# The edge masks of a graph kernel are loaded in five parts, each with its own semaphore

## The chip, the cores and the metric

One core of one Trainium2 chip runs the whole program. The metric is device microseconds (us) of one execution; lower is better. The kernel before took 2149.53 us (median of 3 runs, 2148.34 to 2161.56).

The core has five engines with an instruction queue each: TensorE (PE; its weight loads are shown as PEld), VectorE (DVE), ScalarE (ACT), GpSimd (POOL) and SyncE (SP). An engine runs its own instructions in order and waits for the others on semaphores. SP here does nothing but issue transfers (DMAs) between the device memory and the on-chip memory; sixteen DMA engines carry them out.

## The reference: what is computed

50,000 nodes with 128 features each, 12,500 edges sorted by their destination. A first graph convolution, then four layers of graph attention; each of the five adds something to a node from its few incoming edges, and most nodes have none. Cut to what matters:

```python
def _L0_gnn_ref(...):
    msg = node[edge_src] * edge_weight[:, None]
    N_h = segment_sum(msg, edge_dst, num_segments=N_NODES) * in_sqrt_degree
    out = (entity_embed + N_h) @ W_weight.T + W_bias
    return where(out >= 0, out, NEG_SLOPE * out)

def _gat_layer(x, src, dst, ea, W, We, a_s, a_d, a_e, b, g, beta):
    h = x @ W
    alpha = leaky_relu((h @ a_s)[src] + (h @ a_d)[dst] + (ea @ We) @ a_e, 0.2)
    alpha = _segment_softmax(alpha, dst, N)
    out = segment_sum(h[src] * alpha[:, None], dst, num_segments=N) + b
    return layernorm(out) * g + beta

x = x + _L0_gnn_ref(relu(layernorm(x)), ...)
h = relu(layernorm(x))
x = x + (four times _gat_layer, starting from h)
```

The sums over edges of one destination (`segment_sum`) are what the edge masks are for.

## The kernel before, in words

**Edges.** The edges are cut into 100 tiles (`C`) of 125 edges (`P`), and the tiles are worked on two at a time: 50 pairs (`NU`). `S` holds the rows of the source nodes of all edges, `T` those of the destination nodes. In each tile a mask of 125 x 125 says which edges have the same destination; `M` holds the 100 masks in bf16, 12,500 values (25,000 bytes) on each of 125 partitions. For a pair, `mask(n)` multiplies two masks by the weights of their edges into one of four slots (`MA`, `NS` = 4), and TensorE multiplies the rows in `S` by them, which sums edges of one destination.

**Nodes.** The dense part works on all nodes in 100 groups of 500, read from the input into a ring of 12 buffers (`X`, `XS` = 12) and written to the output from there. It is cut into five shares of 36, 16, 16, 16 and 16 groups.

**Stages.** The program is: setup; masks made and stored to memory (`m_t`); `dense` with 36 groups; `conv_layer` over the 50 pairs; and then four times `dense` with 16 groups and `attention(l)`. `attention(l)` has two blocks: first a softmax over all edges, a chain of small operations that goes back and forth between VectorE, TensorE and ScalarE; then a loop over the 50 pairs like that of `conv_layer`. All five engines meet at a barrier at the end of each block.

**Why the masks come back.** The ring `X` and the masks `M` lie on the same bytes (both begin at the start of `R`). So each `dense` overwrites the masks, and they are read back from `m_t` behind it: once at the start of the block of `conv_layer` (line 1266), and once in the softmax block of each `attention(l)` (line 1650), where SP also waits for them to land before it goes to the barrier. In `conv_layer` it is `mask(0)` on VectorE that waits for them (line 1461).

**Transfers.** `dma2` (lines 171 to 173) issues each transfer as two: partitions 0 to 111, and 112 to 124. The two add 16 each to one semaphore, so that 32 says that both have landed.

**Order on the engines.** The loops over pairs are software pipelines: in step `t` each engine does operation `op` for pair `t - lag`, in the order in which `run_slot` is given them. On VectorE in `conv_layer`, in step 2, `mask(0)` stands behind the first steps' statistics, and everything later on VectorE stands behind it. SP issues in `conv_layer` first the masks, and then for each pair a store of its rows once they are ready.

Of the kernel before, what the change touches and what calls it, by code (L numbers as in the profile page):

```python
# [6 lines left out]
BF16 = mybir.dt.bfloat16  # L7
# [8 lines left out]
P = 125  # L16
C = E // P
# [7 lines left out]
XS = 12  # L25
# [8 lines left out]
def gnn_kernel(nc, x, src, dst, ea, ew, w0, b0, wg, we, att_s, att_d, att_e, bg, gamma, beta, out):  # L34
    ctx = ExitStack()
    with ctx:
# [5 lines left out]
        def sem(name):  # L42
            return ctx.enter_context(nc.semaphore(name))
# [12 lines left out]
        def signal(*names):  # L56
            for n in names:
                if n not in signals:
                    signals[n] = Signal(n)
            got = [signals[n] for n in names]  # L60
            return got if len(got) > 1 else got[0]
# [11 lines left out]
        R = RB[0:P]  # L73
# [6 lines left out]
        M = R[:, 0:P * C // 2].bitcast(BF16).rearrange("p (c e) -> p c e", c=C)  # L80
# [82 lines left out]
        row_t = nc.dram_tensor("row_t", [P * TC, RW], F32, kind="Internal").ap()  # L163
        x1_t = nc.dram_tensor("x1_t", [P * TC, D], F32, kind="Internal").ap()
        m_t = nc.dram_tensor("m_t", [P, C * P], BF16, kind="Internal").ap()
        row_v = row_t.rearrange("(p c) f -> p c f", p=P)
        x1_v = x1_t.rearrange("(p c) f -> p c f", p=P)
        x_v = x.rearrange("(i p r) f -> i p r f", p=P, r=Q)
# [2 lines left out]
        def dma2(eng, dst_ap, src_ap, s):  # L171
            eng.dma_start(dst_ap[0:CORE], src_ap[0:CORE]).then_inc(s, 16)
            eng.dma_start(dst_ap[CORE:P], src_ap[CORE:P]).then_inc(s, 16)
# [665 lines left out]
        def dense(first_group, groups, moves, move, arrive):  # L839


            loaded = [signal(f"x_loaded_{s}") for s in range(XS)]
            stored = [signal(f"out_stored_{s}") for s in range(XS)]
            (counted1, var1, rooted1, inverted1, scaled1, y1_vector, y1_scalar, turned1, copied1, conv_done, sloped,
             leaked, joined, counted2, var2, rooted2, inverted2, scaled2, y2_vector, y2_scalar, turned2, copied2,
             beta_added) = signal(
# [390 lines left out]
        def first_moves(pool, a, b):  # L1237
            gather_x(pool, T, dstI, a, b, s_xdst)

        dense(0, SHARES[0], TC, first_moves, [(s_xsrc, 16 * C), (s_xdst, 16 * TC)])  # L1240

        s_ml = sem("masks_loaded")
        s_x1 = sem("x1_stored")
        s_rows = sem("rows_stored")
        STORE = 5
# [2 lines left out]
        def conv_layer():  # L1248
# [14 lines left out]
            with nc.Block() as block:  # L1263
                @block.sync
                def _(sp):
                    dma2(sp, R[:, 0:P * C // 2].bitcast(BF16), m_t, s_ml)
                    for n in range(NU):
                        sp.wait_ge(*beta_added.at(n + 1))
                        dma2(sp, x1_v[:, 2 * n:2 * n + 2, :], XB[:, n % NS, :, :], x1_kept[n % NS].s)
                        if n % STORE == STORE - 1:  # L1270
                            sp.wait_ge(*score_kept.at(n + 1))
                            dma2(sp, row_v[:, 2 * (n + 1 - STORE):2 * n + 2, :], T[:, 2 * (n + 1 - STORE):2 * n + 2, :], s_rows)
                    sp.wait_ge(*x_stage.at(10))
                    sp.dma_start(x1_v[0:C, C, :], END[:, :]).then_inc(s_x1, 16)
                    sp.wait_ge(*x_stage.at(12))
                    sp.dma_start(row_v[:, C, :], T[:, C, :]).then_inc(s_x1, 16)
                    sp.wait_ge(s_x1, 32)
                    for k in range(NS):
                        sp.wait_ge(*x1_kept[k].at(32 * ((NU - k + NS - 1) // NS)))
                    sp.wait_ge(s_rows, 32 * STORES)  # L1280
# [142 lines left out]
                def _(dve):  # L1423
# [33 lines left out]
                        return op  # L1457

                    def mask(n):
                        if n == 0:  # L1460
                            dve.wait_ge(s_ml, 32)
                        if n >= NS:
                            dve.wait_ge(*gathered.at(n - NS + 1))
                        nc.vector.tensor_tensor(MA[:, n % NS, :, :], M[:, 2 * n:2 * n + 2, :],
                                                alphaS[:, 2 * n:2 * n + 2].unsqueeze(2).broadcast_to([P, 2, P]),
                                                ALU.mult).then_inc(masked.s, 1)
# [26 lines left out]
                    for t in slots:  # L1493
                        run_slot(t, NU, [(0, statistics1), (8, keep_scores), (6, scale2), (7, copy2), (5, statistics2), (0, aggregate1), (6, edge), (5, aggregate2), (1, invert1), (2, mask), (4, leak), (1, scale1), (5, invert2)])
# [37 lines left out]
            x_stage.base += 12  # L1532
            x_act.base += 5
            x_pe.base += 5

        conv_layer()

        s_refresh = sem("s_refreshed")
# [9 lines left out]
        def attention(l):  # L1548
# [7 lines left out]
            with nc.Block() as block:  # L1556
# [90 lines left out]

                @block.sync
                def _(sp):
                    dma2(sp, R[:, 0:P * C // 2].bitcast(BF16), m_t, s_ml)  # L1650
                    sp.wait_ge(s_ml, 32 * (l + 2))

            segbox[0].end()
            act_in.base += 1
# [18 lines left out]
            with nc.Block() as block:  # L1673
# [146 lines left out]
                def _(dve):  # L1820
                    def mask(n):
                        r = n % NS
                        if n >= NS:
                            dve.wait_ge(*gathered.at(n - NS + 1))
                        nc.vector.tensor_tensor(MA[:, r, :, :], M[:, 2 * n:2 * n + 2, :],  # L1825
                                                alphaS[:, 2 * n:2 * n + 2].unsqueeze(2).broadcast_to([P, 2, P]),
                                                ALU.mult).then_inc(masked.s, 1)
# [57 lines left out]
                    for t in slots:  # L1885
                        run_slot(t, NU, [(0, diagonal), (0, mask), (4, rescale_t), (3, invert), (1, edge)] if final else [(0, mask), (2, add_bias_t), (1, add_bias_s), (0, copy_s), (4, edge)])
# [23 lines left out]
                sig.base += NU  # L1910
            for sig in (squared, rooted, inverted) if final else (turned, turned_copied, next_done, bias_t, bias_s):
                sig.base += NU
            scaled.base += NU + 1 if final else 0
            x_stage.base += 4 if final else 3
            x_act.base += 2 if final else 1
# [3 lines left out]
        for l in range(L):  # L1919
            dense(done, SHARES[l + 1], C, refresh, [(s_refresh, 16 * C * (l + 1))])  # L1920
            done += SHARES[l + 1]
            attention(l)
# [23 lines left out]
```

## Time and profile before

| what | value |
|---|---|
| median of 3 runs | 2149.53 us |
| all three | 2149.53, 2148.34, 2161.56 us |
| the profiled execution | 2153.21 us |
| its span, first to last instruction | 2151.5 us |
| mean granted TensorE clock | 0.868 of full speed |
| PE / PEld busy | 1598.8 us (74%) / 1206.1 us (56%) |
| DVE busy | 1633.3 us (76%) |
| ACT busy | 1543.9 us (72%) |
| POOL busy | 1060.0 us (49%) |
| SP's transfers, all | 116.60 MB, 19.5% of 16 DMA engines |

The profiled execution is 3.68 us above the median, and 1.71 us of its time lie outside its span. Busy shares are means over stages that differ: no engine is busy all the time, and what a change is worth has to be read at the place where it acts. Times in the views are counted from the start of the span; a "<-" behind an idle time names what ended it. A queue with a q (SPq, DVEq, PEq) is the engine's sequencer, which issues transfers and takes part in barriers.

### The profile page before, as it was taken

The page shows a single profiled execution, that of the slowest core. Times are in us where ns is not written, and L with a number is a line of the kernel's source. Part 1 is how long each engine was busy: PE and PEld are TensorE (multiplying, and loading weights), DVE is VectorE, ACT ScalarE, POOL GpSimd, SP SyncE. Part 2 cuts the span into 40 slices and gives each one's busy share as a digit, 9 for nine tenths or more (in the row PEclk, how much of TensorE's full clock was granted, in tenths as well). Part 3 has the DMA queues.
Part 4 walks back from the last instruction along what each step waited for, and adds up shares of the span by engine and source line. Part 5 has one row for each costly group of instructions (what it writes and reads, how often), then busy time and mean ns, then how long its engine had stood idle before and what let it go on. Part 6 is the DMA issues. An engine that isn't in the chain of part 4 may idle for free. (4 is left out here: it accounts for less than half of the span.)

```text
span 2151.5 us, 40995 instructions
## 1 busy us (share of the span) xinstructions
PE 1598.8 (74%) x9595; PEld 1206.1 (56%) x9595; DVE 1633.3 (76%) x8491; ACT 1543.9 (72%) x7842; POOL 1060.0 (49%) x919
## 2 busy tenths in 40 slices
PE   2589488888658886787597885796883996884960
PEld 1589355555347775454496552794542994542850
DVE  3581489999769996798686896786895786985960
ACT  0362199999659995798497995696993896992640
POOL 0477778600035553877003786005774007772877
PEclk9996599999879997799697997897996997995985
DMA  8013323311122112221323122223113123213421
GB/s 150 19 40 98 96 53 97 102 59 49 39 76 66 58 52 72 58 59 48 82 67 107 25 59 71 66 64 90 44 44 93 50 67 77 58 40 105 105 66 35
DMA packets 123136, 145.44 MB, mean 68 GB/s; under 512 B 56197, under 2 KB 83637, under 8 KB 122145
## 3 DMA queue, kind: packets, MB, share of 16 engines
q1 hardware_dynamic: 66303, 116.60, 19.5%
q0 software_dynamic: 56160, 25.44, 5.9%
q8 instruction: 78, 1.28, 0.3%
q14 instruction: 163, 1.34, 0.2%
q10 hardware_dynamic: 432, 0.79, 0.1%
HBM read 94.80 MB, written 68.06 MB: 76 GB/s over the span
## 5 line engine op out<-in xcount | busy, mean ns | idle before, releaser
L217 POOL DMA_INDIRECT S<-row_t,rowI x400 | 540.0, 1350 | 573.1 <-issue 573.1
L951 PE MATMUL bank<-AC,XT 128*125 128x390 f32 x800 | 326.3, 513 | 0.4
L1015 ACT ACTIVATE R<-bank 125x128 f32<-125x128 f32 x1200 | 320.8, 301 | 0.0
L1015 ACT ACTIVATION_READ_ACCUMULATOR R<-bank 125x1 f32 x1200 | 274.6, 236 | 0.0
L1741 PE MATMUL bank<-WCX,XT 128*125 128x130 f32 (+1 forms) x1400 | 218.4, 279 | 0.1
L205 PEld LDWEIGHTS bank<-ident,Y 125*128 125x128 f32 x800 | 97.9, 150 | 212.5 <-issue 137.6
L205 PE MATMUL bank<-ident,Y 125*128 125x125 f32 x800 | 131.1, 289 | 113.4 <-ACT XT L999 52.0
L1057 DVE BATCH_NORM_STATS2 st<-R 125x6 f32<-125x128 f32 x800 | 173.2, 279 | 33.2 <-issue 32.7
L217 POOL DMA_INDIRECT S<-in_x,srcI x100 | 131.3, 1313 | 111.9 <-issue 111.9
L1741 PEld LDWEIGHTS bank<-WCX,XT 128*125 128x125 f32 x1400 | 182.4, 188 | 6.8 <-ACT XT L1778 0.5
L931 PEld LDWEIGHTS bank<-AC,XT 128*125 128x125 f32 x800 | 104.6, 202 | 118.1 <-ACT SB L1032 111.6
L931 PE MATMUL bank<-AC,XT 128*125 128x128 f32 x800 | 123.8, 301 | 59.1 <-ACT SB L1032 55.4
L1720 PE MATMUL bank<-R,S 125*128 125x125 f32 x800 | 159.0, 281 | 6.4 <-DVE T L1882 3.2
L221 POOL DMA_INDIRECT out_rows<-T,repNI x101 | 123.5, 1223 | 74.3 <-DVE T L1882 43.1
L1722 PE MATMUL bank<-R,T 125*128 125x125 f32 x800 | 157.7, 279 | 0.0
L217 POOL DMA_INDIRECT T<-in_x,dstI x101 | 136.9, 1356 | 41.7 <-issue 41.7
L951 PEld LDWEIGHTS bank<-AC,XT 128*125 128x125 f32 x800 | 132.5, 195 | 44.2 <-issue 8.3
L1037 ACT ACTIVATE R<-bank 125x128 f32<-125x128 f32 x400 | 107.5, 311 | 38.1 <-PE bank L935 36.9
L1720 PEld LDWEIGHTS bank<-R,S 125*128 125x128 f32 x800 | 124.1, 195 | 8.6 <-issue 6.1
L212 PE MATMUL bank<-W,R 128*125 128x128 f32 x800 | 128.8, 310 | 0.0
L1768 ACT ACTIVATE R<-ident,aselfS 125x125 f32<-125x125 f32 x300 | 109.0, 439 | 23.2 <-PEq L1556 23.2
L1722 PEld LDWEIGHTS bank<-R,T 125*128 125x128 f32 x800 | 124.6, 196 | 0.0
(449 smaller groups left out, 4907.3 us busy)
## 6 DMA issues: line engine op xcount, KB each, us to landing
row_t<-T SPq DMA_DIRECT2D x40, 573.1 KB
R<-in_x SPq DMA_DIRECT2D x100, 224.0 KB
out_rows<-R SPq DMA_DIRECT2D x100, 224.0 KB
R<-m_t SPq DMA_DIRECT2D x5, 2734.4 KB
S<-row_t,rowI POOLq DMA_INDIRECT x400
T<-in_edge_attr SPq DMA_DIRECT2D x1, 5600.0 KB
x_t<-XB SPq DMA_DIRECT2D x50, 112.0 KB
R<-x_t SPq DMA_DIRECT2D x25, 224.0 KB
```

The source lines that it names most:

```text
L205: ins = nc.tensor.transpose(ps[:, a * P:(a + 1) * P], t, ident[0:P, 0:P])
L212: ins = nc.tensor.matmul(pz[0:P, a, :], xt[:, a * P:(a + 1) * P], w, start=False, stop=True, skip_group_check=True)
L217: pool.indirect_dma_start(to, None, table, bass.IndirectOffsetOnAxis(ap=idx, axis=0), bounds_check=rows - 1, oob_is_err=False).then_inc(do ...
L221: pool.indirect_dma_start(table, bass.IndirectOffsetOnAxis(ap=idx, axis=0), frm, None, bounds_check=rows - 1, oob_is_err=False).then_inc(d ...
L931: nc.tensor.matmul(last_of(g)[:, a, :], h0(g, a), AC[3], start=a == 0, stop=False, skip_group_check=True)
L951: nc.tensor.matmul(LAYERS[a][0:P, 0:3 * D + 6], h0(g, a), ACB[:, 0:3 * D + 6], start=True, stop=True).then_inc(layers_done.s, 1)
L1015: ins = nc.scalar.activation(JUNK[:, a * 3 + l, :], LAYERS[a][0:P, l * D:(l + 1) * D], ACT.Square, scale=D ** -0.5, accum_out=NRM[:, g % N ...
L1057: ins = nc.vector.bn_stats(ring[:, a, :], v[:, a, :])
L1720: nc.tensor.matmul(o, S[:, 2 * n + a, 0:D], MA[:, r, a, :], start=True, stop=False, skip_group_check=True)
L1722: ins = nc.tensor.matmul(o, T[:, 2 * n + a, 0:D], DGB[:, r, a, :], start=False, stop=True, skip_group_check=True)
L1741: ins = nc.tensor.matmul(product(banks[bank + r], 2 * P)[:, a, :], XT[:, r, xt + a * P:xt + (a + 1) * P], WCX[:, l, 0:cols], start=not fin ...
L1768: ins = nc.scalar.activation(DGB[:, n % NS, a, :], ident[0:P, 0:P], ACT.Copy, scale=aselfS[:, 2 * n + a:2 * n + a + 1])
```

## The change

Both places that read the masks back now call `load_masks`: five transfers of 20 tiles each (5,000 bytes on each partition) in place of one of 100, each again in two by `dma2`, with five semaphores. `mask(n)` waits, at n = 0, 10, 20, 30 and 40, for the part in which its pair lies, in `conv_layer` and in all four attention layers. SP no longer waits for the masks at the end of the softmax block. The ring's semaphores get other names, and five of them are used for the masks too (the ring is at rest then).

```diff
         m_t = nc.dram_tensor("m_t", [P, C * P], BF16, kind="Internal").ap()
+        m_v = m_t.rearrange("p (c e) -> p c e", c=C)
...
-            loaded = [signal(f"x_loaded_{s}") for s in range(XS)]
-            stored = [signal(f"out_stored_{s}") for s in range(XS)]
+            loaded = [signal(f"ring_loaded_{s}") for s in range(XS)]
+            stored = [signal(f"ring_stored_{s}") for s in range(XS)]
...
-        s_ml = sem("masks_loaded")
+        MC = C // 5
+        masks_loaded = [signal(f"ring_loaded_{s}") for s in range(5)]
+
+        def load_masks(sp):
+            for k in range(5):
+                dma2(sp, M[:, k * MC:(k + 1) * MC, :], m_v[:, k * MC:(k + 1) * MC, :], masks_loaded[k].s)
+
+        def wait_masks(dve, n):
+            if 2 * n % MC == 0:
+                dve.wait_ge(*masks_loaded[2 * n // MC].at(32))
+
+        def masks_used():
+            for s in masks_loaded:
+                s.base += 32
...
                 @block.sync
                 def _(sp):
-                    dma2(sp, R[:, 0:P * C // 2].bitcast(BF16), m_t, s_ml)
+                    load_masks(sp)
                     for n in range(NU):
...
                     def mask(n):
-                        if n == 0:
-                            dve.wait_ge(s_ml, 32)
+                        wait_masks(dve, n)
                         if n >= NS:
                             dve.wait_ge(*gathered.at(n - NS + 1))
...
                 @block.sync
                 def _(sp):
-                    dma2(sp, R[:, 0:P * C // 2].bitcast(BF16), m_t, s_ml)
-                    sp.wait_ge(s_ml, 32 * (l + 2))
+                    load_masks(sp)
...
                     def mask(n):
                         r = n % NS
+                        wait_masks(dve, n)
                         if n >= NS:
                             dve.wait_ge(*gathered.at(n - NS + 1))
```

SP's queue at the start of `conv_layer`: before, the two issues of the whole masks (112 and 13 partitions of 12,500 values), and then the first pair's store.

```order
-L1264 UNCONDITIONAL_BRANCH [waits barrier_Pool_Activation_PE_DVE_SP_release]
-L172 DMA R<-m_t 112x12500
-L173 DMA R<-m_t 13x12500
-L172 DMA x_t<-XB 112x256 [waits addend_added]
-L173 DMA x_t<-XB 13x256
```

The same place now: ten issues of 2,500 values on a partition each. The last of the five parts is shown with the store behind it.

```order
+L1279 UNCONDITIONAL_BRANCH [waits barrier_Pool_Activation_PE_DVE_SP_release]
+L173 DMA R<-m_t 112x2500
+L174 DMA R<-m_t 13x2500
+L173 DMA R<-m_t 112x2500
+L174 DMA R<-m_t 13x2500
+L173 DMA R<-m_t 112x2500
+L174 DMA R<-m_t 13x2500
+L173 DMA R<-m_t 112x2500
+L174 DMA R<-m_t 13x2500
+L173 DMA R<-m_t 112x2500
+L174 DMA R<-m_t 13x2500
+L173 DMA x_t<-XB 112x256 [waits addend_added]
```

Eight issues have come in ahead of the first store; the order is otherwise the same.

VectorE at pair 10 of `conv_layer`, before: the mask multiplication (output and input both lie in `R`) between a reciprocal and the maximum of the leaky rectifier.

```order
L1449 RECIPROCAL rr<-rt 125x4 [waits root1]
L1464 TENSOR_TENSOR R<-R,alphaS 125x250 [waits aggregated]
L1476 TENSOR_TENSOR Y<-Y,bank 125x512 [waits slope_ready]
L1455 SCALAR_TENSOR_TENSOR nm<-mv,rr 125x4 [waits inverse1]
L1449 RECIPROCAL rr<-rt 125x4 [waits root2]
```

The same place now (line numbers are higher by 15 here):

```order
L1464 RECIPROCAL rr<-rt 125x4 [waits root1]
L1478 TENSOR_TENSOR R<-R,alphaS 125x250 [waits aggregated,ring_loaded_1]
L1490 TENSOR_TENSOR Y<-Y,bank 125x512 [waits slope_ready]
L1470 SCALAR_TENSOR_TENSOR nm<-mv,rr 125x4 [waits inverse1]
L1464 RECIPROCAL rr<-rt 125x4 [waits root2]
```

No instruction has moved; the multiplication waits for a second semaphore. That is so at pairs 10, 20, 30 and 40 of each of the five loops; at pair 0 of `conv_layer` the wait for `masks_loaded` has become one for `ring_loaded_0`.

## Rows read from the trace of the kernel before

**Rows 1.** Timeline at the start of `conv_layer`: start us, length us, engine, line, operation.

```profile
594.54 0.32 SPq L172 DMA_DIRECT2D R<-m_t  x1
594.91 0.39 SPq L173 DMA_DIRECT2D R<-m_t  x1
...
598.49 0.15 DVE L1449 RECIPROCAL rr<-rt 125x4 f32<-125x4 f32 x1
598.95 0.28 ACT L1372 ACTIVATE rt<-mv,epsc 125x4 f32<-125x4 f32 x1
610.60 0.42 DVE L1464 TENSOR_TENSOR R<-R,alphaS 125x250 f32<-125x250 bf16 x1 [11.96 <-DMA R<-m_t]
...
611.12 0.65 PE L1321 MATMUL bank<-ident,Y 125*128 125x125 f32 x2 [24.93 <-DVE R L1464]
611.12 0.88 ACT L1383 ACTIVATE Y<-S,nm,rr 125x128 f32<-125x128 f32 x2 [11.89 <-DVE nm L1455]
```

**Rows 2.** Waits of VectorE in `conv_layer`: us in total, times, longest us.

```profile
DVE R L1464 <- DMA R<-m_t: 12.0, 1, 12.0
DVE Y L1476 <- ACT Y L1395: 6.5, 7, 2.7
DVE S L1487 <- PE bank L1345: 3.8, 2, 1.9
```

**Rows 3.** Busy time by stretch: PE, PEld, DVE, ACT, POOL, clock, DMA share, GB/s.

```profile
595.00:607.00 12.00, 0.00 (x0) 0.00 (x0) 3.47 (x31) 2.39 (x7) 1.84 (x4) 0.50 1.04 262
...
607.00:607.50 0.50, 0.00 (x0) 0.00 (x0) 0.00 (x0) 0.00 (x0) 0.00 (x0) 0.50 0.02 0
...
609.00:610.00 1.00, 0.00 (x0) 0.00 (x0) 0.00 (x0) 0.00 (x0) 0.00 (x0) 0.50 0.01 0
...
634.00:639.00 5.00, 4.44 (x34) 3.76 (x35) 5.00 (x33) 5.00 (x15) 3.11 (x6) 1.00 0.11 31
```

**Rows 4.** Timeline at the start of the dense stages: first ring load, first use.

```profile
250.22 0.32 SPq L172 DMA_DIRECT2D R<-in_x  x1
250.59 0.39 SPq L173 DMA_DIRECT2D R<-in_x  x1
251.03 0.34 SPq L172 DMA_DIRECT2D R<-in_x  x1
...
253.32 0.29 DVE L1057 BATCH_NORM_STATS2 st<-R 125x6 f32<-125x128 f32 x1 [11.29 <-issue]
...
857.25 0.33 SPq L172 DMA_DIRECT2D R<-in_x  x1
857.63 0.38 SPq L173 DMA_DIRECT2D R<-in_x  x1
...
860.10 0.29 DVE L1057 BATCH_NORM_STATS2 st<-R 125x6 f32<-125x128 f32 x1 [5.39 <-issue]
```

**Rows 5.** Transfer issues by line, with KB each (the two parts of `dma2`).

```profile
R<-in_x SPq DMA_DIRECT2D x100, 224.0 KB
R<-m_t SPq DMA_DIRECT2D x5, 2734.4 KB
R<-in_x SPq DMA_DIRECT2D x100, 26.0 KB
R<-m_t SPq DMA_DIRECT2D x5, 317.4 KB
```

**Rows 6.** Waits of SP's queue over the whole span.

```profile
SPq L1556 <- DMA R<-m_t: 59.4, 4, 15.0
SPq L1556 <- PEq L1556: 24.8, 4, 7.0
```

**Rows 7.** The same, in the stretch that holds the softmax of layer 0.

```profile
SPq L1556 <- DMA R<-m_t: 14.9, 1, 14.9
SPq L1556 <- PEq L1556: 4.0, 1, 4.0
```

**Rows 8.** Timeline of layer 0: masks issued, and first use behind the barrier.

```profile
1032.66 0.32 SPq L172 DMA_DIRECT2D R<-m_t  x1
1033.03 0.39 SPq L173 DMA_DIRECT2D R<-m_t  x1
...
1052.61 0.42 DVE L1825 TENSOR_TENSOR R<-R,alphaS 125x250 f32<-125x250 bf16 x1 [0.30 <-PEq L1556]
```

**Rows 9.** Mask multiplications of `conv_layer`, all 50: ns min/median/max, first and last start.

```profile
L1464 DVE TENSOR_TENSOR R<-R,alphaS x50: 376/382/419, 610.6 to 824.8; 125x250 f32<-125x250 bf16 x50
```

**Rows 10.** Timeline: the mask multiplications of pairs 3 and 4, first store.

```profile
620.33 0.30 SPq L172 DMA_DIRECT2D x_t<-XB  x1
...
621.07 0.39 DVE L1464 TENSOR_TENSOR R<-R,alphaS 125x250 f32<-125x250 bf16 x1
...
626.64 0.38 DVE L1464 TENSOR_TENSOR R<-R,alphaS 125x250 f32<-125x250 bf16 x1
```

**Rows 11.** Stretches as in rows 3, where the TensorE clock rises: `conv_layer`, layer 0.

```profile
620.00:622.00 2.00, 2.00 (x9) 1.75 (x9) 1.46 (x15) 0.00 (x0) 0.86 (x2) 0.50 0.22 64
622.00:624.00 2.00, 2.00 (x12) 1.95 (x11) 1.01 (x6) 1.64 (x5) 0.25 (x1) 0.58 0.00 0
624.00:626.00 2.00, 0.94 (x7) 0.58 (x6) 1.98 (x13) 2.00 (x6) 1.92 (x4) 1.00 0.00 0
...
1056.00:1058.00 2.00, 2.00 (x15) 2.00 (x15) 1.14 (x4) 0.52 (x3) 0.00 (x0) 0.71 0.00 0
```

**Rows 12.** Span of the core and its mean granted TensorE clock.

```profile
core 0: 2151.5 us, clock 0.868
```

**Rows 13.** Semaphore instructions of VectorE's queue at line 1556: ns min/median/max.

```profile
L1556 DVEq EVENT_SEMAPHORE  x4: 21/21/21, 1052.5 to 1976.7; - x4
```

**Rows 14.** Timeline: the shortest operation that VectorE does.

```profile
598.22 0.06 DVE L196 MEMSET taken<- 125x1 f32 x1
```

More of the change, by code:

```diff
@@ L1534, in conv_layer @@
             x_pe.base += 5
+            masks_used()
         conv_layer()
@@ L1912, in attention @@
                 sig.base += NU
+            masks_used()
             scaled.base += NU + 1 if final else 0
```

## The prediction

> **What bounds the kernel now.** No single engine does, so I read by place. The masks come back at five places, and the question at each is what ends last there: the transfer or something else.
>
> I began with VectorE's waits in `conv_layer`. The reader should see one entry that has nothing like it beside it: 12.0 us, once, at the mask multiplication, ended by the transfer from `m_t` [rows 2]. The timeline gives the place. SP issues the masks at 594.54; VectorE has done its last instruction ahead of the wait at 598.49 + 0.15 = 598.64; the multiplication starts at 610.60 [rows 1]. Everything else stands still behind it: ScalarE's first normalisation of the next pair and TensorE's first transposes both start at 611.12, one for the bias that VectorE computes behind the mask, the other for the mask itself [rows 1]. GpSimd has done its first diagonals (1.84 us in the stretch), and from 607 to 610.6 no engine and hardly a packet moves [rows 3]. So this wait is on the path, with nothing beside it.
>
> Then the four softmax blocks. SP waits there for the masks 59.4 us in four times, and afterwards for the barrier 24.8 us in four times [rows 6]. The second number is the one that matters: in every layer SP is at the barrier early. The tightest is layer 0, where it waits 14.9 us for the transfer and then 4.0 us for the others [rows 7]; 24.8 - 4.0 leaves 6.9 us each for the other three. The transfer is hidden behind the softmax chain in all four.
>
> Last, the steady state of `conv_layer`: in 634 to 639 both VectorE and ScalarE are busy 5.00 of 5 us [rows 3]. A start that is earlier by some time is then an end that is earlier by the same time, since the loop waits for nothing outside itself: its rows of `T` and `S` are there at the start, and SP only stores.
>
> **The change, part by part.**
>
> *The first wait of `conv_layer`.* Before, the data took 610.60 - 594.54 = 16.06 us from SP's first issue to the multiplication, for 2734.4 + 317.4 KB [rows 1, 5], that is 3.125 MB. Now 0.625 MB have to land. No transfer of that size is waited for in this trace, so I bound it from transfers that are. A ring load of 224.0 + 26.0 KB (0.256 MB) [rows 5] is used 253.32 - 250.22 = 3.10 us after its issue in the first dense stage and 860.10 - 857.25 = 2.85 us in the second, with others queued behind it both times [rows 4]. Between 2.98 us at 0.256 MB and 16.06 us at 3.125 MB a line has 4.56 us per MB, and gives 2.98 + 0.369 x 4.56 = 4.66 us. The masks would be there at 599.20, and the wait would be 599.20 - 598.64 = 0.56 us. I take that.
>
> Early end: 2.85 us or less would be there before VectorE asks, and the wait would be 0. Late end: the part's second issue ends at 594.91 + 0.39 = 595.30; at the 262 GB/s of the whole load [rows 3] its packets take 2.39 us more, to 597.7; and behind the last packets of the whole load, about 607, it took 3.6 us until VectorE went on [rows 1, 3]. If that tail is the same for a small part, it is there at 601.3, and the wait is 2.7 us. So the wait shrinks by 11.96 - 0.56 = 11.4 us, between 9.3 and 12.0.
>
> The Trainium skill, "DMA: Bandwidth & Descriptors", section "Anatomy of one DMA", has a fit of 2.0 us plus bytes over 436 GB/s for a transfer issued by GpSimd. By it the whole load would take 9.2 us, where the trace has 16.06, and the first part 3.4 us, an estimate by that page. Then the wait would be nothing and the gain 11.96 instead of 11.4. The measurement is against the fit at the large end, so the sum stays with the line between two rows.
>
> *The later parts.* A ring load's two issues stand 0.81 us apart from the next load's [rows 4], so all ten mask issues are out by about 594.54 + 5 x 0.83 = 598.7. SP's next work, the first store, was issued at 620.33 [rows 10] and comes 11 us earlier at most, at 609: it is not delayed. The load as a whole should end where it did, near 610. Part 1 is asked for at pair 10. Pair 4 was at 626.64 [rows 10], the last of the 50 at 824.8 [rows 9], so a pair takes (824.8 - 626.64) / 45 = 4.40 us, and pair 10 comes at 653, or at 642 if all moves by 11. That is over 30 us behind the last part. No later wait costs anything.
>
> *The four attention layers.* First use is at the barrier's end, 1052.61 - 1032.66 = 19.95 us after the issue [rows 8], against 4.7 us for the first part and about 16 for the last. SP's wait was over 4.0 us before the barrier [rows 7], so its removal gives 0. If the cover were gone, the cost would be the transfer's excess over some 20 us, and only for the part that pair needs.
>
> *The new waits.* Pairs 10, 20, 30 and 40 of five loops wait for a second semaphore, 20 times. What a second wait costs on VectorE no row shows; the nearest are a semaphore instruction of its queue, 21 ns [rows 13], and its shortest operation, 60 ns [rows 14]. Below, 0, if it is checked while the engine works on. That gives 0 to 1.2 us; I take 20 x 0.021 = 0.4, since it is a semaphore instruction. The names of the ring's semaphores cost nothing: the same counts at the same places.
>
> *TensorE's clock.* The stall ended at the low level, 0.50, which is 1.2 GHz, and the clock rose at about 623.7, 12.6 us after the first transposes; in layer 0 it rose within about 5 us of its start at 1052.6 [rows 1, 8, 11]. At the low level a pair took 626.64 - 621.07 = 5.57 us instead of 4.40 [rows 10], so a us of it costs 1 - 4.40 / 5.57 = 0.21 us. I take the rise to come as long after the start as before (0), with 8 us sooner (1.7 us gained) and about 5 later (1.0 lost) as ends.
>
> *The sum.* 11.96 - 0.56 - 0.4 = 11.0 us. From the profiled execution, 2153.21 us (span 2151.5), that is 2142.2. The median of the runs is 3.7 us below the profiled one, and from it the sum is 2149.53 - 11.0 = 2138.5 us. The ends: 12.0 + 1.7 = 13.7 gained, and 11.96 - 2.7 - 1.2 - 1.0 = 7.1 gained, which is 2135.8 to 2142.4. The profiled execution lies 3.7 us from the median of the three runs; taking that either way for the scatter of a median gives 2132 to 2146.
>
> **The rivals.**
>
> *The first part lands with the rest.* If the DMA engines worked on the five parts by turns, or told of the first only when the later ones are done, VectorE would wait until about 610 as before, and the time would be 2149.5 + 0.4, or 2150 us. For it speaks that all ten issues are out within about 4 us, before any is complete, and that the load's end was told of 3.6 us after its last packets. Against it, both ring loads of [rows 4] had others queued behind them, and were usable in 3 us. The same page of the Trainium skill, "Queues, rings and completion order", says that each DMA engine takes a queue's descriptors in order, though completions may come out of order. In between lies a part that is slowed by half of the queue behind it, 5 us of wait, 2143.
>
> *Small transfers are slower.* Rows of 5,000 bytes instead of 25,000 could lower the rate. The ring's rows have 2,048 bytes, and load well [rows 4]. Even if the whole took twice as long, 32 us, part k (from 0) is there after 6.4 (k + 1) us, and only the first is waited for: from 598.64 to 594.54 + 6.4 = 600.9, 2.3 us in place of 0.56, which is 2140. The skill's rule in "Rules for kernel authors" of that page, to batch transfers to 1 MiB or more, speaks against the change; here it can reach only this one part.
>
> *The wait is traded for TensorE's clock, and it ends slower.* The core runs at a mean of 0.868 [rows 12], so about (1 - 0.868) / 0.5 x 2151.5 = 568 us of the span are at the low level. All stages behind begin 11 us earlier, and if their stretches at the low level grew, each us would cost about 0.21. From 52 us more (11.0 / 0.21) the gain is gone; 150 us more would give 2138.5 + 31.5 = 2170, slower by 1%. For it: one of the three runs was 12 us above the median with nothing changed. Against it: the order of work is the same everywhere, and a shorter stall is not more rest for TensorE.
>
> **How the numbers follow.** A measurement of this kernel can tell about 1% (21 us) from no change. Forecast (gain 7 to 14 us): 0.80. First part late or with the rest: 0.08. Rate halved, else as forecast: 0.03. Clock, slower than before in any amount: 0.07, of which 0.03 by over 1%. Gain of more than the waits explain, by the clock: 0.02. The whole stall is 12 us, 0.56%, so that faster by over 1% has only the last case: 0.02; slower by over 1% 0.03; within 1% 0.95. The range 2132 to 2146 holds the forecast and the half late part, and leaves out the case without gain and most of the slower ones.
>
> **What would show it.** In the profile after: VectorE's wait for the masks in `conv_layer` at 0.2 to 2.7 us instead of 12.0; the multiplication starting 4 to 7 us after SP's first mask issue; a distance from there to the last of the 50 within 2 us of 214.2 (824.8 - 610.6) [rows 9]; no wait for a mask at pairs 10 to 40, nor at any in the attention layers; SP waiting for the barrier some 19 us instead of 15 and 4; the first use in layer 0 still 20 us after the issue. I am wrong if the first part's wait stays above 3 us, if the loop from first to last mask grows by what was gained, or if a later stage lengthens.

## The result, and the profile after

The changed kernel takes 2137.84 us (median of 20 runs) against 2149.66 us for the kernel before (20 runs): a ratio of 0.9947, 95% interval 0.9935 to 0.9959, which is 8.8 to 14.0 us less. The forecast was 2138.5 us.

The timeline at the start of `conv_layer`, after (start us, length us, engine, line, operation), which answers to [rows 1]:

```profile
593.84 0.33 SPq L173 DMA_DIRECT2D R<-m_t  x1
594.23 0.39 SPq L174 DMA_DIRECT2D R<-m_t  x1
...
596.98 0.14 DVE L1464 RECIPROCAL rr<-rt 125x4 f32<-125x4 f32 x1
...
597.90 0.42 DVE L1478 TENSOR_TENSOR R<-R,alphaS 125x250 f32<-125x250 bf16 x1 [0.78 <-DMA R<-m_t]
...
598.42 0.65 PE L1336 MATMUL bank<-ident,Y 125*128 125x125 f32 x2 [13.74 <-DVE R L1478]
```

The first two lines are the issues of the second part; the first part's are these, from the same view a little earlier:

```profile
593.02 0.32 SPq L173 DMA_DIRECT2D R<-m_t  x1
```

So the first part is used 597.90 - 593.02 = 4.88 us after its issue (16.06 before), and VectorE waits 0.78 us for it instead of 11.96. The other four parts are still on their way then: with the order reversed, below, the fifth part is used 14.9 us after the first issue. VectorE's waits in `conv_layer` (us in total, times, longest), to be held beside [rows 2]:

```profile
DVE Y L1490 <- ACT Y L1410: 6.6, 7, 2.7
DVE S L1501 <- PE bank L1360: 3.8, 2, 1.9
...
DVE R L1478 <- DMA R<-m_t: 0.8, 1, 0.8
```

What headed the list has gone to its end, and the other entries are the same within 0.1 us: no wait has taken its place. The loop behind it has not changed either. All 50 mask multiplications (ns min/median/max, first and last start), for [rows 9]:

```profile
L1478 DVE TENSOR_TENSOR R<-R,alphaS x50: 376/384/421, 597.9 to 812.1; 125x250 f32<-125x250 bf16 x50
```

812.1 - 597.9 is 214.2 us, the same as 824.8 - 610.6. In the attention layers SP now only waits for the barrier, where it waited for the transfer and then for the barrier [rows 6]:

```profile
SPq L1571 <- PEq L1571: 70.3, 4, 18.6
```

The span fell by more than the wait did, from 2151.5 to 2135.6 us, 15.9 us. Where that lies shows in the length of each stage, counted from SP's first transfer of a stage to its first of the next. A layer begins where its masks are issued, and the softmax of layer 3 ends where that layer begins to read back the rows that it adds to:

```
us                     setup  dense0  conv   dense1 layer0 dense2 layer1 dense3 layer2 dense4 softmax3  rest
before                 250.2  344.3   262.7  175.4  129.1  176.5  131.5  176.5  132.7  175.1   22.7    174.7
after                  248.0  345.0   251.6  175.5  129.4  174.1  132.7  174.9  132.4  175.1   22.7    174.2
```

`conv_layer` has 11.1 of it. Setup, which the change does not reach, has 2.2, and the others together 2.6, up and down by 2.4 at most. These are the scatter of one execution: another profile of the same changed kernel (the first experiment) has 250.0 for setup and 348.2 for the first dense stage, and a span of 2142.1. What a single pair of spans differs by beyond the wait is therefore not the change's.

### The profile page after: what moved, and what is told of

The parts are those of the page before. It is cut to its first block and busy times, and to the rows that moved or that the text cites. A ratio compares the mean times of both kernels' runs of the same rounds, so it can differ in the third digit from the quotient of the medians.

```text
span 2135.6 us, 41051 instructions
## 1 busy us (share of the span) xinstructions
PE 1596.4 (75%) x9595; PEld 1203.5 (56%) x9595; DVE 1634.7 (77%) x8491; ACT 1545.1 (72%) x7842; POOL 1053.8 (49%) x919
## 5 line engine op out<-in xcount | busy, mean ns | idle before, releaser
L206 PEld LDWEIGHTS bank<-ident,Y 125*128 125x128 f32 x800 | 97.5, 149 | 213.6 <-issue 136.2
L1734 PEld LDWEIGHTS bank<-R,S 125*128 125x128 f32 x800 | 125.5, 198 | 11.2 <-issue 8.8
```

What stands on the lines that cost most here:

```text
L206: ins = nc.tensor.transpose(ps[:, a * P:(a + 1) * P], t, ident[0:P, 0:P])
L1734: nc.tensor.matmul(o, S[:, 2 * n + a, 0:D], MA[:, r, a, :], start=True, stop=False, skip_group_check=True)
```

## The experiments

All times are medians beside runs of the kernel before on the same chip: 2148.85 us for the changed kernel again, only `conv_layer` split, ten parts, and a wait at every pair; 2150.29 us for only attention split, the reversed order, and the two late loads; 2149.68 us for two parts and the small first part. Line numbers differ by a few between kernels.

**The changed kernel again** (no edit).

> The changed kernel itself, beside the next three on one chip. Theory (the whole gain is the first mask wait of conv_layer, 12.0 us before and 0.8 us in the first profile of after): 11.2 us faster than the kernel before, near 2138; VectorE's wait for the masks in conv_layer 0.5 to 1.0 us, first to last mask multiplication 214.2 us. Rival (part of the gain of the medians, 11.8 us, comes from later stages): the stages behind conv_layer are shorter than before by 1 us or more here too.

Measured: 2140.52 us (12 runs), ratio 0.9966 (0.9948 to 0.9983). In its profile:

```profile
602.91 0.42 DVE L1478 TENSOR_TENSOR R<-R,alphaS 125x250 f32<-125x250 bf16 x1 [0.64 <-DMA R<-m_t]
...
L1478 DVE TENSOR_TENSOR R<-R,alphaS x50: 377/382/419, 602.9 to 817.3; 125x250 f32<-125x250 bf16 x50
```

The wait is 0.64 us and the loop 214.4. The gain on this chip is 8.3 us, 3 us less than the wait gives, and in the first comparison it was 11.8. The 11.2 us lie inside the first interval (8.8 to 14.0) and just at the edge of this one (3.7 to 11.2). The stages behind `conv_layer` take 1293.0 us together, where the kernel before has 1294.2 and the first profile of after 1291.0. By its own bar of 1 us that would speak for the rival. But the next kernels show that this sum does not go with the change: it is 1289.9 us with no attention layer split, and 1294.7 in the kernel with the reversed order, which has all four split.

**Only `conv_layer` split.** In attention:

```diff
-                    load_masks(sp)
+                    load_whole(sp)
+                    sp.wait_ge(*whole.at(32))
...
-                        wait_masks(dve, n)
```

> Only the load of conv_layer is split; the four attention layers load the masks whole, SP waits for them in the softmax block, and no mask multiplication of attention waits. Theory (the gain is the one wait of conv_layer): the same time as with all five split, 11 us faster than before, within 2 us of e0. Rival (the attention layers gain from the load that is no longer waited for, 0.5 us or more each): 2 us or more slower than e0.

Measured: 2139.08 us, ratio 0.9952 (0.9939 to 0.9965), and a wait of 0.91 us at the first mask. The whole gain is there without the attention layers.

**Only the attention layers split.** In `conv_layer`:

```diff
-                    load_masks(sp)
+                    load_whole(sp)
                     for n in range(NU):
...
-                        wait_masks(dve, n)
+                        if n == 0:
+                            dve.wait_ge(*whole.at(32))
```

> The load of conv_layer is whole again, waited for at pair 0; the four attention layers are split as in the change. Theory (the gain is the one wait of conv_layer): no gain, within 2 us of the kernel before, VectorE waits 12 us for the masks in conv_layer. Rival (the attention layers gain too): faster than before by 2 us or more.

Measured: 2149.95 us, ratio 1.0011 (0.9985 to 1.0036), with two of the twelve runs at 2169.11 and 2175.90 us. The wait is back:

```profile
594.27 0.32 SPq L173 DMA_DIRECT2D R<-m_t  x1
...
610.77 0.42 DVE L1485 TENSOR_TENSOR R<-R,alphaS 125x250 f32<-125x250 bf16 x1 [12.40 <-DMA R<-m_t]
```

The two halves of the change are thus told apart: 12.4 us of wait and no gain with one, 0.9 us and the whole gain with the other. Four fifths of the edited transfers bring nothing measurable.

**The parts of `conv_layer` issued from the last to the first.**

```diff
-        def load_masks(sp):
-            for k in range(5):
+        def load_masks(sp, order=range(5)):
+            for k in order:
...
-                    load_masks(sp)
+                    load_masks(sp, range(4, -1, -1))
                     for n in range(NU):
```

> Five parts, but conv_layer's are issued from the last to the first, so that the part of pair 0 is fifth in SP's queue. Theory (parts land in the order in which they are issued, at about 262 GB/s all together): pair 0's part lands with the end of the whole load, about 15 us after the first issue; VectorE waits 11 us, and the time is that of the kernel before, 2149. Rival (the DMA engines work on the parts by turns, and a part's landing depends little on its place in the queue): the wait is well under 11 us, and some of the gain stays.

Measured: 2150.54 us, ratio 0.9998 (0.9986 to 1.0009). The first issue and the first mask:

```profile
596.14 0.32 SPq L173 DMA_DIRECT2D R<-m_t  x1
...
611.01 0.42 DVE L1478 TENSOR_TENSOR R<-R,alphaS 125x250 f32<-125x250 bf16 x1 [10.77 <-DMA R<-m_t]
```

The part that is fifth in the queue is used 14.9 us after the first issue, where the one that is first is used after 4.9. Splitting alone gives nothing; what gives the gain is that the part which is needed first is issued first. This decides the rival by which the parts land together. It also shows that the split load as a whole is not slower than the whole one (16.06 us before, and 610.77 - 594.27 = 16.50 in the kernel above).

**Two parts of 50 tiles.**

```diff
-        MC = C // 5
+        MC = C // 2
...
-            for k in range(5):
+            for k in range(2):
```

> Two parts of 50 tiles (1.5625 MB each), everywhere. It tests the line through two transfers by which the first part was sized (2.98 us + 4.56 us per MB behind 0.256 MB). Theory: the first part lands 2.98 + 1.3065 x 4.56 = 8.9 us after its issue; VectorE asks about 4.1 us after it and waits 4.8 us, 4.0 us longer than with five parts; near 2142.5. Rival (the time to landing has a fixed end of 3.6 us behind the packets, at 262 GB/s): 0.76 + 5.96 + 3.6 = 10.3 us, a wait of 6.2 us.

Measured: 2141.25 us, ratio 0.9961 (0.9948 to 0.9975). In the profile SP issues at 597.28, the first mask starts at 606.7, and VectorE's entry is

```profile
DVE R L1478 <- DMA R<-m_t: 5.3, 1, 5.3
...
597.28 0.32 SPq L173 DMA_DIRECT2D R<-m_t  x1
...
L1478 DVE TENSOR_TENSOR R<-R,alphaS x50: 377/383/419, 606.7 to 820.1; 125x250 f32<-125x250 bf16 x50
```

9.4 us for 1.5625 MB lies between the line's 8.9 and the rival's 10.3, nearer to the line. With 4.9 us at 0.625 MB and 16.06 at 3.125 MB, the time to use is near 2 us plus 4.5 to 4.8 us per MB. The wait is 4.5 us longer than with five parts in the first profile of after; the medians, on different chips, can't tell a difference of that size well: the gain here is 8.4 us, and five parts had 11.8 and 8.3.

**Ten parts of ten tiles.**

```diff
-        MC = C // 5
+        MC = C // 10
...
-            for k in range(5):
+            for k in range(10):
```

> Ten parts of ten tiles in place of five of twenty, everywhere. Theory (a part lands at 2.98 us + 4.56 us per MB behind 0.256 MB, so 0.3125 MB after 3.2 us; VectorE asks 4.1 us after the first issue): no wait for a mask at pair 0, 0.8 us faster than e0, and no later wait, since twenty issues are out in 9 us. Rival (SP's issues or many short transfers cost something): slower than e0 by 1 us or more, or the first part not earlier than with five.

Measured: 2139.48 us, ratio 0.9964 (0.9947 to 0.9982), 12 runs. VectorE has no wait for a mask any more, as expected: the first mask follows the instruction ahead of it at once, 4.0 us after the first issue.

```profile
595.80 0.32 SPq L173 DMA_DIRECT2D R<-m_t  x1
...
599.75 0.15 DVE L1464 RECIPROCAL rr<-rt 125x4 f32<-125x4 f32 x1
599.81 0.39 DVE L1478 TENSOR_TENSOR R<-R,alphaS 125x250 f32<-125x250 bf16 x1
```

The 0.8 us that this could bring are lost in the scatter. But three of its twelve runs took 2153 to 2155 us, and the profiled one is among them (2154.92, span 2153.2, clock 0.861). It shows what such a run is. Its masks go from 599.8 to 832.2, 232.4 us instead of 214.2, and the stretches (us, then PE, PEld, DVE, ACT, POOL busy, granted clock, DMA share, GB/s) read:

```profile
611.00:616.00 5.00, 4.25 (x24) 3.73 (x24) 3.73 (x27) 4.38 (x12) 2.51 (x4) 0.74 0.02 5
616.00:621.00 5.00, 3.62 (x29) 3.16 (x27) 4.64 (x29) 5.00 (x15) 2.52 (x4) 0.94 0.16 47
621.00:626.00 5.00, 5.00 (x22) 4.24 (x22) 3.38 (x18) 3.81 (x12) 2.51 (x4) 0.50 0.09 26
...
651.00:656.00 5.00, 5.00 (x22) 4.25 (x22) 3.04 (x23) 2.48 (x8) 1.74 (x3) 0.50 0.68 206
656.00:670.00 14.00, 14.00 (x70) 12.49 (x71) 9.05 (x60) 9.89 (x26) 5.04 (x8) 0.56 0.07 21
670.00:700.00 30.00, 26.16 (x212) 22.94 (x211) 30.00 (x200) 30.00 (x83) 17.62 (x28) 1.00 0.15 45
```

TensorE's clock rises to its upper level (2.4 GHz) at about 613.6, falls back to the lower (1.2 GHz) at about 620.4, while TensorE works, and stays there until about 668.2. In that stretch TensorE is busy all the time and VectorE about two thirds of it; from 670 VectorE is busy all the time and TensorE 87% of it. The mask multiplications of two neighbouring pairs inside it give the price:

```profile
634.02 0.39 DVE L1478 TENSOR_TENSOR R<-R,alphaS 125x250 f32<-125x250 bf16 x1
...
641.16 0.39 DVE L1478 TENSOR_TENSOR R<-R,alphaS 125x250 f32<-125x250 bf16 x1
```

A pair takes 7.14 us there instead of 4.40, so a us at the low clock costs 1 - 4.40 / 7.14 = 0.38 us, and 48 us of it cost 18, which is the whole of the 232.4 - 214.2.

The busy times ahead of the fall do not explain it. Here are the 6.8 us between the rise and the fall, and behind them the 6.8 us that follow the rise in the kernel before, where the clock stayed up to the end of the loop:

```profile
613.60:620.40 6.80, 4.67 (x36) 3.87 (x35) 6.42 (x42) 6.80 (x19) 4.45 (x8) 1.00 0.07 22
...
623.70:630.50 6.80, 4.36 (x33) 3.49 (x33) 6.42 (x40) 6.80 (x20) 4.79 (x8) 1.00 0.06 19
```

**A wait at every pair.**

```diff
         def wait_masks(dve, n):
-            if 2 * n % MC == 0:
-                dve.wait_ge(*masks_loaded[2 * n // MC].at(32))
+            dve.wait_ge(*masks_loaded[2 * n // MC].at(32))
```

> The wait for the part stands at every pair, not at every tenth: 225 further waits on VectorE, all on semaphores that have long been reached. It prices the second wait, of which the change has 20. If it costs what VectorE's semaphore instruction takes (21 ns): 4.7 us slower than e0, near 2143. If it is checked while the engine works (0): as e0. If it costs as much as the shortest operation (60 ns): 13.5 us slower.

Measured: 2139.57 us, ratio 0.9962 (0.9949 to 0.9974), beside 2140.52 for the change on the same chip. The loop of `conv_layer`, which has 45 of the 225 further waits, is not longer:

```profile
L1477 DVE TENSOR_TENSOR R<-R,alphaS x50: 376/383/420, 601.6 to 814.6; 125x250 f32<-125x250 bf16 x50
```

213.0 us against 214.2 and 214.4 is not a fair comparison, though: here TensorE's clock rose 8.3 us after its first transposes, and in those two profiles 12.8 and 12.3 us after them. The kernel with only `conv_layer` split, whose clock rose after 8.4 us, is the one to compare with:

```profile
L1484 DVE TENSOR_TENSOR R<-R,alphaS x50: 376/383/420, 601.7 to 814.9; 125x250 f32<-125x250 bf16 x50
```

That is 213.2 us without the further waits. A second wait on a semaphore that has been reached costs nothing that can be seen here. 13.5 us is excluded; 4.7 is unlikely by the medians, and by the loop (45 x 21 ns would be 0.9 us more, not 0.2 less).

**The attention loads issued late, in parts.**

```diff
                 def _(sp):
+                    sp.wait_ge(*act_out.at(2))
                     load_masks(sp)
```

> As the change, but in each attention layer SP issues the masks only when both exponentials of the softmax are done, some 8 us before the block's end instead of 20. Theory (the attention loads were hidden, and a first part needs 4.9 us): still hidden, within 2 us of the change, near 2138, no mask wait over 0.5 us in attention. Rival (the split brings nothing in attention even without cover): slower by what e8 is slower.

Measured: 2140.73 us, ratio 0.9944 (0.9932 to 0.9956): the same gain as the change's. In layer 0:

```profile
1033.80 0.32 SPq L173 DMA_DIRECT2D R<-m_t  x1
...
1041.49 0.42 DVE L1841 TENSOR_TENSOR R<-R,alphaS 125x250 f32<-125x250 bf16 x1 [0.30 <-PEq L1571]
```

The first mask is used 7.7 us after the issue, at once behind the barrier. By the 15 us that all five parts took with the reversed order, the last ones are still landing then, and no mask multiplication in attention waits for them.

**The same, as one whole load** that SP waits for at the block's end.

```diff
-                    load_masks(sp)
+                    sp.wait_ge(*act_out.at(2))
+                    load_whole(sp)
+                    sp.wait_ge(*whole.at(32))
...
-                        wait_masks(dve, n)
```

> As e7, but the attention layers load the masks whole, and SP waits for them at the end of the softmax block as in the kernel before (conv_layer split). Theory (15.3 us from the second issue to landing, of which some 8 us are covered): each of the four layers waits 8 us for SP at the barrier, 4 x 8 = 32 us slower than e7, near 2170. Rival (the cover is larger than the chain of waits shows): under 20 us slower than e7.

Measured: 2179.27 us, ratio 1.0144 (1.0116 to 1.0172), 38.5 us slower than in parts by the medians, and 2171.5 - 2139.7 = 31.8 by the two spans profiled. The waits of SP's queue and the first use in layer 0:

```profile
SPq L1577 <- DMA R<-m_t: 62.4, 4, 15.9
...
1046.12 0.42 DVE L1847 TENSOR_TENSOR R<-R,alphaS 125x250 f32<-125x250 bf16 x1 [9.66 <-PEq L1577]
```

VectorE now stands 9.66 us before the barrier lets it go. So the attention layers gain nothing from the split only because a softmax chain of some 20 us lies over the load; with 8 us of cover, the split is worth over 30 us in four layers. The expected 32 are met by the spans. The profiles show where most of the rest is: from issue to first use the four layers take 17.0, 16.7, 16.8 and 17.0 us here, and 7.7, 8.1, 7.7 and 8.1 in parts, 35.9 us more in all. The other 2.6 us of the medians are within the scatter of six runs each.

**A small first part** of 4 tiles, and four of 24.

```diff
-        MC = C // 5
+        BOUNDS = (0, 4, 28, 52, 76, C)
...
-                dma2(sp, M[:, k * MC:(k + 1) * MC, :], m_v[:, k * MC:(k + 1) * MC, :], masks_loaded[k].s)
+                dma2(sp, M[:, BOUNDS[k]:BOUNDS[k + 1], :], m_v[:, BOUNDS[k]:BOUNDS[k + 1], :], masks_loaded[k].s)
...
-            if 2 * n % MC == 0:
-                dve.wait_ge(*masks_loaded[2 * n // MC].at(32))
+            if 2 * n in BOUNDS:
+                dve.wait_ge(*masks_loaded[BOUNDS.index(2 * n)].at(32))
```

> Five parts in all, the first of 4 tiles (0.125 MB), four of 24 behind it. Candidate for a version that beats both: no mask wait at all in conv_layer, ten issues only. Theory (only the wait counts): 0.8 us faster than five equal parts, near 2137.5, no wait at pair 0 or at pair 2. A second question is open from the ten-part kernel, three of whose twelve runs were 15 us longer, by a fall of TensorE's clock early in conv_layer: if that hangs on the loop starting without a mask wait, several runs of this kernel are near 2154 too; if it is chance, about one in twenty, as before and with five parts.

Measured: 2138.36 us, ratio 0.9951 (0.9931 to 0.997), 12 runs. No wait for a mask anywhere:

```profile
596.49 0.14 DVE L1464 RECIPROCAL rr<-rt 125x4 f32<-125x4 f32 x1
...
596.55 0.39 DVE L1478 TENSOR_TENSOR R<-R,alphaS 125x250 f32<-125x250 bf16 x1
...
L1478 DVE TENSOR_TENSOR R<-R,alphaS x50: 377/383/391, 596.6 to 812.7; 125x250 f32<-125x250 bf16 x50
```

The loop is 216.1 us in this profile, 1.9 more than in the two of before and after, so here the 0.8 us did not come through. The clock accounts for it. It rose 7.8 us after the first transposes (597.1), fell back 6.8 us later, and was low for another 10.2 us:

```profile
604.90:611.70 6.80, 4.35 (x33) 3.64 (x33) 5.87 (x45) 5.40 (x16) 4.41 (x8) 1.00 0.26 71
611.70:622.00 10.30, 10.02 (x45) 8.62 (x43) 7.08 (x41) 7.88 (x22) 5.02 (x8) 0.50 0.11 31
```

That is 18.0 us at the low level instead of the 12.8 of the first profile of after, and 5.2 us more of it at 0.38 are 2.0 us. The kernel does not beat the change by anything that can be measured. One run of twelve took 2159 us. Whether a loop that starts without a wait makes the long fall of the clock likelier stays open: of runs above 2150 us, this kernel has 1 in 12, ten parts 3 in 12, and the changed kernel 1 in 20 and 1 in 12.

A wider count asks whether the change itself does. Taking a run as long when it is over 10 us above the median of its kernel, the kernels whose `conv_layer` is split in order have 7 long runs in 83, and the kernel before 1 in 83. But the kernel with only attention split, whose `conv_layer` is as before, has 2 in 12, and the reversed order none in 12. That is a hint and no more. If it holds, 8% of long runs at some 17 us each take back about 1.4 us of the mean gain, not of the median.

## Why the prediction was right, point by point

- **What bounds.** That the 11.96 us in front of the first mask were on the path with nothing beside them held. The loop kept its 214.2 us, the stage lost 11.1 us, and no other wait of VectorE grew. The comparison is a clean one, since TensorE's clock rose 12.5 us after the first transposes before, and 12.8 us after them in the changed kernel.
- **When the first part lands.** The step was a line between two transfers of other sizes: 4.66 us forecast, 4.88 measured (4.7 to 5.2 in the other profiles with five equal parts), and a wait of 0.78 us (0.64 to 1.12) where 0.56 was forecast. The late bound, which took the 3.6 us behind the last packets for a fixed tail, was too careful for a small part; two parts of 50 tiles came between it and the line. The Trainium skill, "DMA: Bandwidth & Descriptors", section "Anatomy of one DMA", has a fit for transfers issued by GpSimd, and the estimate by it was no wait at all. For these transfers, issued by SP, the traces do not agree: 0.78 us of wait were measured, and 9.4 us for 1.5625 MB, where an estimate by that fit is 5.6.
- **The parts land in the order of issue.** The rival had a chance of 0.08; with the order reversed it was the part's place in the queue that decided, 14.9 us for the fifth against 4.9 for the first.
- **Small transfers are slower.** Not here: all five parts were in after 14.9 us, where the whole load took 16.1 (16.5 in the kernel with only attention split), and ten parts or a first part of 4 tiles left no wait.
- **The later parts and SP's queue.** No wait at pairs 10 to 40. The first store is issued at 607.64, when it is ready, far behind the last mask issue at 597.06.
- **The attention layers give 0.** Shown from both sides: split alone there, no gain; left whole there, no loss. SP's wait at the barrier in layer 0 was forecast at some 19 us and is 15.2; over the four layers it is 70.3 us, where 59.4 + 24.8 = 84.2 stood before. The difference is some 3.5 us a layer, since ten issues take SP over 4 us, not 0.7.
- **The new waits** were mis-sized: 0.4 us for 20, taken from a semaphore instruction. (They are 24: the mask multiplication of pair 0 waits too in each attention layer.) With 225 more the kernel was not slower, so the term is 0 as far as can be seen.
- **The clock.** That it would rise as long after the start as before held in the profile after (12.5 us before; after, from 598.4 to about 611.2, 12.8). It was partly luck: over the twelve profiles it rose 12.2 to 13.3 us after the first transposes in five, and 6.6 to 8.4 us in seven. In six of these seven (all but the small first part) the loop is 213.0 to 213.6 us instead of 214.2 to 214.4. So the forecast's early end was real, and worth about 1 us. The price was wrong: 0.21 us for a us at the low level came from 5.57 - 4.40 us over the pair from 621.07 to 626.64, but that pair was at the low level only until 623.7 [rows 10, 11], 2.6 of its 5.57 us. In the full loop the price is 0.38. The rival that ends slower was therefore nearer than it was told: the gain is gone from 29 us more at the low level (11.2 / 0.38), not from 52, and one of the profiled runs had 48 in one piece. In the medians it did not show.
- **The sum.** 11.0 us forecast; 11.2 by the wait, 11.1 by the stage, 11.8 by the medians of 20 runs. The terms that were off by 0.2 and 0.4 us went opposite ways. That the median came within 0.7 us of the forecast is luck beyond that: the same kernel gained 8.3 us on another chip.

## What to carry to other kernels

A transfer that is waited for as a whole, at a point where nothing else can run, is worth splitting by order of use, with the part needed first at the head of the queue; the gain is the landing time of the whole less that of the first part (16.1 - 4.9 = 11.2 us here), at most the wait, and once, however many such transfers there are elsewhere. Before splitting a load, look at what waits for it: the same edit was worth 11 us at one place and nothing at four, because there the chain beside the load was longer than the load. The same split kept its value in reserve: with less cover it saved over 30 us.

## What the runs showed of the hardware that was not expected

TensorE's granted clock can fall from 1.00 back to 0.50 some 7 us after it rose, in the middle of a loop. In the profile of the ten parts TensorE had been busy 4.67 of the 6.8 us before the fall, more than the 4.36 of the same stretch in the kernel before, where nothing fell; then it was busy throughout, and the clock stayed low for 48 us. That cost 18 us at once, more than the whole change gives. In `conv_layer` the clock fell 6.8 us after its rise in six of the twelve profiles: for 3.4 us in four, for 10.2 in the small first part, and for 48 in the ten parts. Long runs come in several kernels, and each that has its clock on record, 2154.08 us (0.863) of the changed kernel for one, has a lower mean clock than the other runs of its kernel. The 2161.56 us of the kernel before are as far out, but that run's clock is not on record. What starts the fall was not settled.

A second semaphore wait on a VectorE instruction, where the semaphore has long been reached, showed no cost in 225 places (213.0 us for a loop with 45 more of them, 213.2 without).
